# A perceiver layer in one program: who stores the contexts, who scales the probabilities, where the first MLP weights are split

## The reference

```python
# 1: attention over the context, 16 heads, no scaling of the scores
kv_rope = kv_c * cos + rotate_half(kv_c) * sin
q_r = (hidden_q @ Wq.T per head) @ w_kc_q @ W_qr        # weights only: folded into one matrix A
scores = q_r @ (kv_rope @ W_kr).T
attn = softmax(scores)
out = ((attn @ kv_rope) @ w_kc_kv.T) @ Wo.T              # weights only: folded into one matrix G
# 2: hs = layernorm(x, ln_w, ln_b);  mamba2(hs) + gelu(hs @ fc1_w + fc1_b) @ fc2_w + fc2_b
# 3: top-2 of 8 experts plus a shared expert
```

## Time and profile before

| | us |
|---|---|
| median of 3 runs (lowest, highest) | 1058.93 (1056.59, 1060.86) |
| the profiled execution | 1062.47 |
| its span | 1060.7 |
| TensorE busy in the span | 962.8 (91%) |
| VectorE busy | 558.0 (53%) |
| ScalarE busy | 411.8 (39%) |
| GpSimd busy | 456.4 (43%) |

### The profile page before, as it was taken

The page is one execution under the profiler, slowest core; times in us unless marked ns, Lnnn a source line. Parts: engine busy times, 40 slices in busy tenths (PEclk is TensorE's granted clock), DMA queues, the critical chain, the costliest instruction groups (busy, mean ns, idle before and its releaser), DMA issues. The chain is left out here.

```text
span 1060.7 us, 15947 instructions
## 1 busy us (share of the span) xinstructions
PE 962.8 (91%) x5479; PEld 805.7 (76%) x5479; DVE 558.0 (53%) x1058; ACT 411.8 (39%) x954; POOL 456.4 (43%) x471
## 2 busy tenths in 40 slices
PE   4888866899898985999999999899999999999988
PEld 4666645777777764888888888686778899999977
DVE  6333358888888852445444432315977433333335
ACT  2333446776677642333223234453333122222101
POOL 1877854433688532000000300305723979993041
PEclk9999998999999997999999999998999999999999
DMA  6787622111111102323421003412022856671142
GB/s 216 213 244 218 211 75 80 41 36 36 36 36 31 36 6 82 117 79 98 140 70 31 20 27 111 133 30 95 2 82 63 281 181 217 212 220 61 41 139 99
DMA packets 79001, 109.89 MB, mean 104 GB/s; under 512 B 14224, under 2 KB 46992, under 8 KB 78928
## 3 DMA queue, kind: packets, MB, share of 16 engines
q1 hardware_dynamic: 70320, 89.52, 27.0%
q10 hardware_dynamic: 6048, 11.01, 3.1%
q0 software_dynamic: 2560, 8.39, 2.4%
HBM read 83.13 MB, written 25.77 MB: 103 GB/s over the span
## 5 line engine op out<-in xcount | busy, mean ns | idle before, releaser
L43 PE MATMUL psum<-second_xT_hi,mlp_w_hi 128*128 128x512 f32 x272 | 108.1, 398 | 8.4 <-DVE mlp_w_lo L1614 4.5
L44 PE MATMUL psum<-second_xT_lo,mlp_w_hi 128*128 128x512 f32 x272 | 107.8, 396 | 0.0
L45 PE MATMUL psum<-second_xT_hi,mlp_w_lo 128*128 128x512 f32 x272 | 107.4, 395 | 0.0
L1128 POOL TENSOR_TENSOR all_x<-all_x,mlp_raw 128x512 f32<-128x512 f32 x8 | 10.0, 1290 | 183.3 <-DVE all_x L1628 183.3
L2144 ACT ACTIVATE moe_s<-psum 128x352 f32<-128x352 f32 x39 | 18.1, 465 | 155.0 <-PE psum L45 135.5
L43 PEld LDWEIGHTS psum<-second_xT_hi,mlp_w_hi 128*128 128x128 f32 x272 | 51.7, 190 | 21.9 <-DVE mlp_w_lo L1235 5.2
L2210 DVE TENSOR_TENSOR moe_hT_lo<-psum,moe_hT_hi 128x384 fp32r<-128x384 f32 x39 | 21.8, 558 | 82.8 <-ACT moe_hT_hi L2150 82.8
L1584 ACT ACTIVATE mlp_s<-psum,mlp_side 128x512 f32<-128x512 f32 x32 | 21.9, 683 | 109.4 <-PE psum L45 109.4
L43 PE MATMUL psum<-moe_w_hi,moe_tT_hi 128*128 x184 | 61.3, 333 | 0.0
L1628 DVE TENSOR_TENSOR all_x<-all_x,psum 128x512 f32<-128x512 f32 x64 | 44.0, 687 | 32.9 <-PE psum L45 32.3
L44 PEld LDWEIGHTS psum<-second_xT_lo,mlp_w_hi 128*128 128x128 f32 x272 | 51.8, 191 | 11.0
(11 more groups left out here) (337 smaller groups left out, 2889.9 us busy)
## 6 DMA issues: line engine op xcount, KB each, us to landing
mlp_raw<-in_fc SPq DMA_DIRECT2D x16, 512.0 KB, 4.3
kv_all<-all_x SPq DMA_DIRECT2D x28, 256.0 KB, 4.4
far_raw<-in_eg SPq DMA_DIRECT2D x10, 704.0 KB
far_raw<-in_eu SPq DMA_DIRECT2D x10, 704.0 KB
slot_rows<-mix_W SPq DMA_DIRECT2D x23, 256.0 KB, 5.8
slot_out<-far_rows ACTq DMA_DIRECT2D x23, 256.0 KB, 2.3
far_raw<-in_ed SPq DMA_DIRECT2D x10, 512.0 KB
far_rows<-slot_rows ACTq DMA_DIRECT2D x19, 256.0 KB, 2.7
```

Of the source, the lines that this page charges most:

```text
L43: e.matmul(out, hi_l, hi_r, start=first, stop=False)
L44: e.matmul(out, hi_l, lo_r, start=False, stop=False)
L45: return e.matmul(out, lo_l, hi_r, start=False, stop=last)
L1128: pool.tensor_tensor(g["x"][:, t, :], g["x"][:, t, :], b2, ALU.add).then_inc(x_plus, 1)
```

## The change

- `store_context` moves from SP to ScalarE's queue, right behind the copy of the same context.
- In the attention the scaling of the second half of the heads (`normalise`, i = 1) moves from VectorE to GpSimd, where it stands before `rows_lo`; the sums and reciprocals stay on VectorE. `transpose_probs` waits for each engine's half.
- The `rows` of the early tiles move from GpSimd to VectorE: one before the scaling of the first half, one behind it. `aggregate` moves from the beginning of a step to the end of the one before.
- The first group's `w1` is loaded and split at the end of the attention: the load on SP behind the last context, the high part on ScalarE behind its loop, the low part on VectorE in the last step. Its tensors are allocated beside `xT2`. The MLP's TensorE starts with the up-product; the transposes of the last tile come behind its first quarter. `raw2` of group 1 is loaded when `raw2` of group 0 is split.

```diff
@@ -417,19 +417,11 @@
-            def store_context(b):
-                u = b % KVB
-                sp.wait_ge(rot, b + 1)
-                sp.wait_ge(kvT_ok, b + 1)
-                sp.dma_start(d["kv_all"][b], kvx[:, u, :, :, :].rearrange("p a c k -> p (a c k)")).then_inc(kv_out[u], 16)
-
 ...
                     load_tails((b + 3) // 2)
-                if 0 <= b - 2 < B - KEPT:
-                    store_context(b - 2)
             load_n(0)
@@ -567,6 +559,11 @@
+            def store_context(b):
+                u = b % KVB
+                act.wait_ge(kvT_ok, b + 1)
+                act.dma_start(d["kv_all"][b], kvx[:, u, :, :, :].rearrange("p a c k -> p (a c k)")).then_inc(kv_out[u], 16)
+
@@ -590,9 +587,11 @@
                     context_columns(BPP * p)
+                    store_context(BPP * p)
                 keep_features(p, 1)
 ...
                     context_columns(BPP * p + 1)
+                    store_context(BPP * p + 1)
                     keep_a(p + 1)
@@ -600,6 +599,8 @@
                 context_columns(BPP * p + 2)
+                if p + 1 < NP:
+                    store_context(BPP * p + 2)
                 keep_queries(p, 1)
@@ -607,6 +608,8 @@
                 context_columns(BPP * p + 3)
+                if p + 1 < NP:
+                    store_context(BPP * p + 3)
@@ -680,7 +683,7 @@
-def phase_attention(nc, d, g, q, G_hi, G_lo, rows, cols, xT2_hi, xT2_lo):
+def phase_attention(nc, d, g, q, G_hi, G_lo, rows, cols, xT2_hi, xT2_lo, up):
@@ -710,7 +713,9 @@
         c_ready, c_hi_ok, c_ok, o_ready, o_ok = (S_(x) for x in ("c_ready", "c_hi_ok", "c_ok", "o_ready", "o_ok"))
+        pr_far_ok = S_("pr_far_ok")
         stats_ok, wb_in, power_set = S_("stats_ok"), S_("wb_in"), S_("power_set")
+        up_in, up_hi_ok, up_ok = S_("up_in"), S_("up_hi_ok"), S_("up_ok")
         block = ctx.enter_context(nc.Block())
@@ -766,6 +771,9 @@
+            sp.wait_ge(q_ok, B - DONE)
+            sp.dma_start(up.raw1[:], d["fc1"][0]).then_inc(up_in, 16)
+
@@ -782,18 +790,22 @@
                 pool.tensor_tensor(q_lo[:, p, :], q[:, place_of(b), :], q_hi[:, p, :].bitcast(F32), ALU.subtract).then_inc(q_ok, 1)
+            def normalise(b):
+                pool.wait_ge(inv_ok, 2 * (b + 1))
+                of = pr(b)[:, 2:4, :]
+                pool.tensor_tensor(of, of, pair(scale, b, 1).unsqueeze(2).to_broadcast([P, 2, LM]), ALU.mult).then_inc(pr_far_ok, 1)
+
 ...
                     norm.root(pool, EARLY.index(s))
-                    for i in range(2):
-                        norm.rows(pool, EARLY.index(s), i)
                 if s - 1 in EARLY:
 ...
                 if s < B:
+                    normalise(s)
                     rows_lo(s)
@@ -821,7 +833,7 @@
                 for i in range(2):
-                    pe.wait_ge(pr_ok, 2 * b + i + 1)
+                    pe.wait_ge((pr_ok, pr_far_ok)[i], b + 1)
                     for j in (2 * i, 2 * i + 1):
@@ -929,6 +941,8 @@
                     norm.high_part(act, EARLY.index(s - 1))
+            act.wait_ge(up_in, 16)
+            act.activation(up.w1_hi[:, 0, :, :], up.raw1[:], ACT.Copy).then_inc(up_hi_ok, 1)
@@ -948,8 +962,9 @@
                 v.wait_ge(inv_ok, done)
-                of = pr(b)[:, 2 * i:2 * i + 2, :]
-                v.tensor_tensor(of, of, pair(scale, b, i).unsqueeze(2).to_broadcast([P, 2, LM]), ALU.mult).then_inc(pr_ok, 1)
+                if i == 0:
+                    of = pr(b)[:, 0:2, :]
+                    v.tensor_tensor(of, of, pair(scale, b, 0).unsqueeze(2).to_broadcast([P, 2, LM]), ALU.mult).then_inc(pr_ok, 1)
@@ -972,22 +987,31 @@
                 t, k = divmod(s - BPT - 2, BPT)
-                if s in EARLY:
-                    v.wait_ge(stats_ok, EARLY.index(s) + 1)
-                    norm.aggregate(v, EARLY.index(s))
                 if s < B:
 ...
                     maxima(s, 1)
+                if s in EARLY:
+                    if s == EARLY[0]:
+                        v.wait_ge(q_ok, 19 + 1 - DONE)
+                    norm.rows(v, EARLY.index(s), 0)
                 if s < B:
                     normalise(s, 0)
+                if s in EARLY:
+                    norm.rows(v, EARLY.index(s), 1)
                 if 0 <= s - 2 < B:
 ...
                     probs_lo(s - 1)
+                if s == B + 2 + BPT - 1:
+                    v.wait_ge(up_hi_ok, 1)
+                    v.tensor_tensor(up.w1_lo[:, 0, :, :], up.raw1[:], up.w1_hi[:, 0, :, :].bitcast(F32), ALU.subtract).then_inc(up_ok, 1)
                 if t >= 0 and k == BPT - 1:
                     keep_output(t)
+                if s + 1 in EARLY:
+                    v.wait_ge(stats_ok, EARLY.index(s + 1) + 1)
+                    norm.aggregate(v, EARLY.index(s + 1))
@@ -1490,7 +1514,7 @@
-def phase_mlp(nc, d, g, front, norm_rows, make_after):
+def phase_mlp(nc, d, g, front, up, norm_rows, make_after):
@@ -1499,9 +1523,8 @@
         n = Names(nc, ctx, "mlp")
-        raw1 = n.sb("raw1", [P, DC, F])
+        raw1, w1_hi, w1_lo = up.raw1, up.w1_hi, up.w1_lo
         raw2 = n.sb("raw2", [P, MC, D])
-        w1_hi, w1_lo = n.sb("w1_hi", [P, 2, DC, F], F32R), n.sb("w1_lo", [P, 2, DC, F], F32R)
         w2_hi, w2_lo = (a[:, 0:2 * MC, :].rearrange("p (u c) k -> p u c k", u=2) for a in (front.wo_hi, front.wo_lo))
@@ -1520,7 +1543,7 @@
-        own.all_split, own.all_up, own.all_down = NWS * groups, U * groups, TT * groups
+        own.all_split, own.all_up, own.all_down = NWS * groups - 1, U * groups, TT * groups
         after = make_after(n, own)
@@ -1545,13 +1568,15 @@
-
-                wait(sp, w_ok, NWS * k)
+                wait(sp, w_ok, NWS * k - 1)
                 sp.dma_start(raw1[:], d["fc1"][k]).then_inc(in1, 16)
                 sp.dma_start(raw2[:], d["fc2"][k]).then_inc(in2, 16)
-            load(0)
+
+            sp.dma_start(raw2[:], d["fc2"][0]).then_inc(in2, 16)
+            sp.dma_start(raw1[:], d["fc1"][1]).then_inc(in1, 16)
             after.sync_first(sp)
-            load(1)
+            sp.wait_ge(w_ok, 1)
+            sp.dma_start(raw2[:], d["fc2"][1]).then_inc(in2, 16)
             for k in range(2, groups):
@@ -1567,10 +1592,10 @@
             def split(k, p):
-                act.wait_ge(in1, 16 * (k + 1))
-
                 wait(act, dn_ready, TT * (k - 1))
-                act.activation(w1_hi[:, p, :, :], raw1[:], ACT.Copy).then_inc(w_hi_ok, 1)
+                if not is_first(k):
+                    act.wait_ge(in1, 16 * k)
+                    act.activation(w1_hi[:, p, :, :], raw1[:], ACT.Copy).then_inc(w_hi_ok, 1)
                 act.wait_ge(in2, 16 * (k + 1))
@@ -1610,9 +1635,10 @@
                 v.tensor_copy(side[:, p, :], b_all[:, bass.ds(k, 1), :]).then_inc(side_ok, 1)
-                v.wait_ge(w_hi_ok, NWS * k + 1)
-                v.tensor_tensor(w1_lo[:, p, :, :], raw1[:], w1_hi[:, p, :, :].bitcast(F32), ALU.subtract).then_inc(w_ok, 1)
-                v.wait_ge(w_hi_ok, NWS * (k + 1))
+                if not is_first(k):
+                    v.wait_ge(w_hi_ok, NWS * k)
+                    v.tensor_tensor(w1_lo[:, p, :, :], raw1[:], w1_hi[:, p, :, :].bitcast(F32), ALU.subtract).then_inc(w_ok, 1)
+                v.wait_ge(w_hi_ok, NWS * (k + 1) - 1)
                 v.tensor_tensor(w2_lo[:, p, :, :], raw2[:], w2_hi[:, p, :, :].bitcast(F32), ALU.subtract).then_inc(w_ok, 1)
@@ -1649,7 +1675,8 @@
             def group(k, p):
-                pe.wait_ge(w_ok, 1 if is_first(k) else NWS * (k + 1))
+                if not is_first(k):
+                    pe.wait_ge(w_ok, NWS * (k + 1) - 1)
                 for half in range(NHALF):
@@ -1663,8 +1690,10 @@
                         last.then_inc(up_ready, 1)
+                        if is_first(k) and m == 0:
+                            norm.transpose(pe, 0, BANK)
                 if is_first(k):
-                    pe.wait_ge(w_ok, NWS)
+                    pe.wait_ge(w_ok, 1)
                 for t in range(TT):
@@ -1673,7 +1702,6 @@
                     last.then_inc(dn_ready, 1)
-            norm.transpose(pe, 0, BANK)
             loop(pe, group)
@@ -2291,10 +2319,14 @@
     m = Names(nc, ctx, tag, side="right")
-    return m.sb("xT_hi", [P, DC, TOK], F32R), m.sb("xT_lo", [P, DC, TOK], F32R)
-
-
-def phase_rest(nc, d, g, edge, xT2_hi, xT2_lo):
+    xT_hi, xT_lo = m.sb("xT_hi", [P, DC, TOK], F32R), m.sb("xT_lo", [P, DC, TOK], F32R)
+    up = Parts()
+    up.w1_hi, up.w1_lo = m.sb("w1_hi", [P, 2, DC, MC * P], F32R), m.sb("w1_lo", [P, 2, DC, MC * P], F32R)
+    up.raw1 = m.sb("raw1", [P, DC, MC * P])
+    return xT_hi, xT_lo, up
+
+
+def phase_rest(nc, d, g, edge, xT2_hi, xT2_lo, up):
     kept = ExitStack()
@@ -2315,7 +2347,7 @@
             once, twice, scaled = (feat[:, 0, i * D:(i + 1) * D] if i < 2 else feat[:, 1, 0:D] for i in range(3))
-            phase_mlp(nc, d, g, front, norm_rows=(once, twice, scaled.rearrange("p (c k) -> p c k", k=P)),
```

(7 more changed lines are left out.)

## The result

The changed kernel takes 1024.6 us (median of 4 runs, 1021.7 to 1027.2) beside 1059.9 for the kernel before on the same chip (4 runs, 1056.6 to 1062.0). The ratio is 0.967, 95% interval 0.963 to 0.971; measured again with the later experiments, 0.967 (0.964 to 0.970). Forecast were 1036.5 with a range of 1023 to 1048. The profiled execution has a span of 1021.1 and took 1022.9.

A forecast was written before the change was run, and what follows sets the result against it. TensorE, nearly always busy, was taken as the bound, so gains come from its idle time: 8 + 3 + 0 + 4 + 7.5 = 22.5, giving 1036.5 for the median; own range 1030 to 1043, with rivals 1023 to 1048.

The forecast's parts named there:

- rival (a): Attention: GpSimd does not hold VectorE up, TensorE bounds the steps, 11 us more are gained: 1025.5; chance 20%.
- Part 1: First stage: context stores on ScalarE's queue end GpSimd's waits for late stores; 8 us gained, ends 0 and 10.
- the 2 that I took off for slower loads: First stage: at most 10.0 us to gain, taken as 8 because loads get a little slower at a higher DMA share.
- Rival (b): First stage: the DMA engines, not SP's order, bound it; moving the stores gives 0 and the time is 1044.5; chance 15%.
- Part 2: Attention: half the scaling on GpSimd gives 0 in plain steps and 3 us over six steps after a kept output.
- Of that size and kind are the rows with 1.28: Attention: GpSimd's new 128x512 scaling instruction was taken to last 1.28 us, like existing rows of its size.
- the walk: Plain attention step, followed through VectorE, ScalarE and GpSimd instruction by instruction: 6.85 us becomes about 6.9.
- the seam: Plain attention step: VectorE's first clamp finds a gap between two GpSimd instructions; the second waits some 1.2 us.
- rival (c): Attention: GpSimd's scaling takes longer than 1.28 us; from 1.9 the kernel is no faster, at 2.07 it takes 1062; chance 5%.
- Part 3: Early tiles' rows on VectorE: zero together in steps 18 to 30, 4 us (3 to 5) at step 34.
- Part 4: MLP's start: first up-weights loaded and split during the attention's end; 7.5 us gained (5.5 to 9.7).
- rival (d): MLP: the up-weights' early split is undone as group 1's second weights wait for a late issue; 1043.5; chance 5%.

The follow-up runs named there:

- e1: The changed kernel with the stores of rotated contexts back on SP behind the loads; ratio 0.978 to the kernel before, first stage 121.7 us.
- e5: The changed kernel with the stores back on SP, each ahead of the load it stood behind; ratio the same as the change's, first stage 114.6 us.
- e9: The changed kernel with GpSimd's scaling replaced by a product with another full SBUF tile; plain step 6.82 us, time 7.5 us longer by the ratios.
- e6: The changed kernel with GpSimd's scaling written as two tensor_scalars of 128x256; plain step 7.37 us, in all 23.5 us longer.
- e2: The changed kernel with the second half of the scaling back on VectorE in all 32 steps; 21 us longer by the ratios, attention 265.1 us.
- e3: The changed kernel with the rows of the early tiles back on GpSimd, the scaling staying there; attention 264.6 us against 264.5 in the kernel before.
- c2: The changed kernel with the clamp as a reduction and the first early tile's scaled columns in a free place; ratio 0.956 to the kernel before.
- e4: The changed kernel with the first up-weights' load and split, and the last tile's transposes, back at the MLP's start; timed 12 us longer (7 to 18).

## Why the prediction was right, and where its sizes were off

The direction, the median within the range and the mechanisms were right; the sum of 22.5 was 12 short, and the forecast's own range of 1030 to 1043 missed. That rival (a) had 1025.5 is chance: it had the clamps free, and they wait 0.59 and 0.62; the sum came out short by other terms, as follows.

- **Part 1, 8 taken, 10 as the end.** e1 makes it 10.2, and from before to after TensorE's waits for rotations fall from 12.9 to 2.7. The two need not agree, and 10.2 in both says little: the idle time fell by 8.9 in all, and 3.1 came from busy time, a term that the prediction, which had TensorE's waits as the most there was to gain, did not have. The mechanism was the one told; the 2 that I took off for slower loads were wrong: at a DMA share of 0.76 GpSimd waited 0.7 + (13.2 - 11.7) = 2.2 for loads in 4 places, and TensorE for none of it. The rest of the 11.8 (1.6) I put down to differences between executions: e1's first stage has before's order and is 1.2 shorter than before's. Rival (b) falls: what was saved was a wait in a queue's order, as e5 shows on SP's own queue. The rule of the Trainium skill that the prediction set against part 1 (DMA: Bandwidth & Descriptors, section "Issuing engines are not separate DMA queues") speaks of the transfers and of the sequencer's time, not of such a wait; so it doesn't foretell the 10.2, and it isn't refuted by them.
- **Part 2, 0 for plain steps and 3 for six others.** The step that failed is "Of that size and kind are the rows with 1.28". The row was 1.04, since it reads one tile and the rows read two. With 1.31 the plain step is 6.82 (e9), close to the walk's 6.85 to 6.9, and the first clamp does find the seam (0.17 at 190.11); with 1.04 it doesn't, and waits 0.59. At 1.31 the step is 0.26 longer and the attention 4.4 longer (255.1 against 250.7; by the ratios, with wide intervals, the time is 7.5 longer). That is most of what parts 2 and 3 gave beyond their 7. After a kept output I had 0.5 to 0.6, and it is 0.53. Of rival (c) the mechanism is right, microsecond for microsecond, and its bound too: it had the kernel no faster from 1.9 on, and at 1.82 e6 is still 1% faster than before.
- **Part 3, 4 at step 34 and zero together in steps 18 to 30.** The end of the attention gives 7.0, steps 17 to 29 give 1.7. I counted the two changes of GpSimd and VectorE in those steps as cancelling, which nearly came true, but at the end both tiles count: the one of step 30, too, was behind 4.14 of GpSimd's. From queries_lo of step 29 to the transposes of that tile it takes 7.74 before and 4.48 after, 3.3 that the sum did not have (either edit alone, e2 or e3, gives 1.4 to 1.5 of them). Behind them 3.7 are gained, and this is the 4 of step 34: 1.3 of it behind the last transposes, where the granted clock was 0.89 and is 1.00. The idle before step 35's transposes is gone as forecast. What I missed is step 19: I named what queues behind the scaling on GpSimd and not that ScalarE waits for its last piece to free a buffer; 2.5 by c2.
- **Part 4, 7.5 taken, 9.7 as the end.** 9.6 by the milestones, 9.1 by e4, both to the first gather. The 7.9 of the start came. The terms I took off it were too large, and the gain from the clock too, 0.9 where I had up to 2.6: the tile's transposes take TensorE 0.35 (393.54 to 393.89), not 1.12, the second half's matmuls wait 0.24, not 1, and the first twelve take 4.4 where they took 5.3. That is 8.2, close to the 8.0 found at the first down-matmul; some 1.4 of the 9.6 I can't place, and they are less than what the stretch to the gather differs by between kernels with the same MLP (385 to 389). So 7.5 is not shown to be too little. No down-matmul waited: rival (d) falls.

## What to carry to other kernels

Two edits that load different engines of one ring are not to be priced one by one: here each alone gave nothing in the attention, and both gave 12.85, since each filled the engine that the other emptied. A transfer that is ready but stands behind one that is not costs what its consumer waits for; look for it in the issuing engine's order before looking at bandwidth. And rows of TensorE that stand back to back don't show that it alone bounds the step, here 6.56 against its own 6.5: look at steps of the same loop in which it has less to do (6.54 here, with TensorE waiting), and see whether they are shorter. A ring that is only as fast as TensorE can't take back what one longer step costs.

## What the hardware did that I had not expected

- A GpSimd tensor_tensor of 128x512 f32 takes 1.04 with one tile read (an operand spread over 256 columns, or the tile itself twice) and 1.28 to 1.31 with two, whether product, sum or difference.
- Two tensor_scalars of 128x256 take 1.82 on GpSimd; the pair of 128x512 with two scalars each 4.14.
- GpSimd's tensor_scalars don't hold VectorE up where its tensor_tensors do. In e3, inside the 4.14 of L218, VectorE's small sum took 0.23 (0.15 without company) and its two-input scaling of 128x512 0.69, as without company; beside L225 the sum took 1.32. VectorE's one-input clamps inside L218 took 0.24 to 0.43 in the kernel before, 0.17 without company: a short wait, not one for the rest of the 2.07 of a single instruction. Why, no run here shows.
- A VectorE tensor_scalar or two-input sum of 128x2, from SBUF to SBUF, waits as long as GpSimd's tensor_tensor has left (up to 1.31 for 0.17 of work); the same clamp as a reduction waits not at all.
